# Three woven columns in an eight-batch Mamba, attention, GLA and MoE kernel: the front of batch t+2 issued during batch t's cycle

## The reference, cut to what matters

```
x = x + mamba(layernorm(x))         # the "scan part"
x = x + ffn(layernorm(x))           # attention, which only modulates a gated MLP
x = x + gla(layernorm(x))           # chunked gated linear attention, 8 chunks of 64
x = x + moe(layernorm(x))           # 32 experts, top 4

mamba: hidden, gate = split(x @ in_proj_w)         # 512 + 512 channels
       u = silu(conv4(hidden) + b)                 # causal, along the tokens
       dt, B, C = rms(split(u @ x_proj_w))         # 128, 16, 16
       dt = softplus(dt @ dt_proj_w + dt_proj_b)
       s_t = exp(dt_t * A) * s_{t-1} + dt_t * u_t * B_t      # 512 channels x 16 states
       y_t = sum over states of s_t * C_t
       out = ((y + u * D) * silu(gate)) @ out_proj_w
```

## Time and profile before

| | us |
|---|---|
| median of 3 runs | 3019.35 |
| lowest, highest | 3016.56, 3025.76 |
| span of the profiled execution | 2958.7 |
| PE busy in it | 2351.0 (79%) |
| DVE busy | 2163.5 (73%) |
| ACT busy | 1383.5 (47%) |
| POOL busy | 575.3 (19%) |

### The profile page before, as it was taken

The page is one execution under the profiler, slowest core; times in us unless marked ns, Lnnn a source line. Parts: engine busy times, 40 slices in busy tenths (PEclk is TensorE's granted clock), DMA queues, the critical chain, the costliest instruction groups (busy, mean ns, idle before and its releaser), DMA issues. The chain is left out here.

```text
span 2958.7 us, 36517 instructions
## 1 busy us (share of the span) xinstructions
PE 2351.0 (79%) x12305; PEld 1420.5 (48%) x12305; DVE 2163.5 (73%) x3017; ACT 1383.5 (47%) x2217; POOL 575.3 (19%) x569
## 2 busy tenths in 40 slices
PE   4448896889778977887788869787879688988991
PEld 2335354535453545444544545345535453556880
DVE  4993898489948894899669975998589852246666
ACT  5323654366535663566356634654465424143440
POOL 4000101120131013111311120212120230025661
PEclk8558897899889987998799979998999789988995
DMA  2320231023201321133113311231033182355757
GB/s 105 120 79 8 103 113 57 15 87 128 74 28 60 128 94 35 42 126 107 42 35 109 117 49 42 92 127 56 8 112 121 60 212 97 103 195 174 219 180 302
DMA packets 136229, 292.85 MB, mean 99 GB/s; under 512 B 14288, under 2 KB 79200, under 8 KB 135792
## 3 DMA queue, kind: packets, MB, share of 16 engines
q1 hardware_dynamic: 122224, 251.96, 26.2%
q0 software_dynamic: 13824, 38.55, 3.6%
HBM read 220.91 MB, written 69.54 MB: 98 GB/s over the span
## 5 line engine op out<-in xcount | busy, mean ns | idle before, releaser
L1367 DVE TENSOR_TENSOR_SCAN scan<-scan 128x1024 f32<-128x1024 f32 x256 | 585.9, 2289 | 34.4 <-ACT scan L1097 26.4
L2047 PE MATMUL bank<-ident,scan 128*128 128x128 f32 x2048 | 325.3, 315 | 168.9 <-DVE scan L1376 158.1
L1097 ACT ACTIVATE scan<-scan 128x511 f32<-128x511 f32 x512 | 337.2, 713 | 164.2 <-DVE scan L1367 163.5
L2047 PEld LDWEIGHTS bank<-ident,scan 128*128 128x128 f32 x2048 | 271.6, 162 | 260.1 <-DVE scan L1376 158.4
L1399 DVE TENSOR_TENSOR scan<-scan 128x1024 f32<-128x1024 f32 x256 | 310.5, 1213 | 29.5 <-PE bank L2047 28.5
L1376 DVE TENSOR_TENSOR scan<-scan 128x1024 f32<-128x1024 f32 x256 | 312.0, 1219 | 7.8 <-DVE rest L1579 7.5
L1936 PE MATMUL bank<-hT,wslot 128*128 128x512 f32 x512 | 246.9, 607 | 0.0
L1541 DVE TENSOR_REDUCE rest<-bank 128x2 f32<-128x1024 f32 (+3 forms) x176 | 196.5, 1126 | 66.5 <-PE bank L2118 63.5
L819 POOL DMA_INDIRECT rows_dram<-stage,slot_at x128 | 164.9, 1288 | 370.4 <-DVE scan L1367 313.1
L1144 ACT ACTIVATE rest<-bank 128x2048 f32<-128x2048 f32 (+3 forms) x128 | 158.2, 1236 | 146.7 <-PE bank L2138 146.6
L1936 PE MATMUL bank<-xT,scan 128*128 128x512 f32 (+1 forms) x352 | 185.0, 672 | 7.4 <-ACT xT L983 4.8
(11 more groups left out here) (341 smaller groups left out, 4231.2 us busy)
## 6 DMA issues: line engine op xcount, KB each, us to landing
scan<-bc_dram SPq DMA_DIRECT2D x256, 512.0 KB, 3.8
wslot<-wt SPq DMA_DIRECT2D x64, 384.0 KB, 3.5
rows_dram<-pad SPq DMA_DIRECT2D x32, 670.0 KB
scan<-y_dram SPq DMA_DIRECT2D x32, 512.0 KB, 10.1
rest<-rows_dram SPq DMA_DIRECT2D x108, 134.0 KB, 2.5
scan<-rows_dram SPq DMA_DIRECT2D x52, 134.0 KB, 2.7
scan<-wt SPq DMA_DIRECT2D x4, 1536.0 KB, 13.6
xa<-x SPq DMA_DIRECT2D x8, 512.0 KB, 3.8
```

The lines of the kernel that those rows point to most:

```text
L1097: i = a.activation(decay[:, unit % 2, n, 1:], dt[:, c, 1:], ACT.Exp, scale=a_neg[:, c, 2 * pair + n:2 * pair + n + 1])
L1367: d.tensor_tensor_scan(flat, decay[:, unit % 2].rearrange("p n t -> p (n t)"), flat, 0.0, ALU.mult, ALU.add).then_inc(decay_used.sem, 1)
L2047: m = t_.matmul(A.bank(("yT", c))[:, t * P:(t + 1) * P], drive[:, unit % NDRIVE, n, t * P:(t + 1) * P], ident[:, :], is_transpose=True, st ...
```

## The change

- The work is split into three columns per engine: U, the units of the scan; R, the rest part; X, the side: the out product of t (`out_part`), tiles 2 and 3 of the softplus and the gate products of t+1 (`gate_part`), the routing of t-1 (`late_alone`) and the front of t+2 (`front_part`: from the load of x to tiles 0 and 1 of dt). A single string of runs for each engine, `ORDER`, names the column and the number of steps, over all turns.
- The front no longer needs the drive buffers. Its tiles lie in `wslot` (`x_f`, `ssm`, softplus), so its load of x waits for the last down product of the MLP that used the slots (`down_done`), and the weights of the next MLP wait for the routing that uses them too. x is loaded a second time into `xa` as residual, 512 KB more for each batch.
- The convolution reads `hid` from PSUM, so its copy to SBUF and the memset go; DVE waits for ACT's first tap instead. `u` of tiles 2 and 3 is double-buffered; y goes into `sgate`; `bc_dram` is doubled.
- PSUM: front, gate, out and routing have rings of their own (F, G, O, K), all in banks 6 and 7 and handed from one to the next; A keeps the transposed y alone.
- The step counts of the U column on DVE are 102 for a turn, of the R column 122.

The core of the diff:

```diff
 def scan_jobs():
-    jobs = [("mT", c, "act") for c in range(NF)] + [("rt", 0, "dve")]
-    ...
-    jobs += [("out", i, "dve") for i in range(2)]
+    jobs = []
+    for c in range(0, NCT, 2): ... yT, y
+def front_jobs(): T, hid, ssm, dtT, bcT, dtp 0 and 1
+def gate_jobs(): dtp 2 and 3, gate
+        x_f = slots[:, 0:NT * HID].rearrange("p (t d) -> p t d", t=NT)
+        K = Ring(sem, "routing_bank", D, late_jobs())
+        F = Ring(sem, "front_bank", D, front_jobs())
+        G = Ring(sem, "gate_bank", D, gate_jobs())
+        O = Ring(sem, "out_bank", D, [(("out", i), "dve", 1) for i in range(2)])
 # SP
+            def front_in(turn):
+                yield
+                if turn >= 2:
+                    sp.wait_ge(down_done.sem, down_done.at(turn - 2, NFT))
+                ...
+                sp.dma_start(x_f, x[turn:turn + 1]...).then_inc(x_in.sem, 16)
 # DVE, convolution
-                        s = sv.step(d.scalar_tensor_tensor(dt[:, c], hid[:, c, k:k + SEQ], conv_w..., dt[:, c], ALU.mult, ALU.add)...)
+                    dve.wait_ge(fa.sem, fa.named(turn, f"tap{c}"))
+                    tile, b = u_of(turn, c), F.bank(("hid", c))
+                        i = d.scalar_tensor_tensor(tile[:, back:], b[:, 0:SEQ - back], conv_w..., tile[:, back:], ALU.mult, ALU.add)
 # DVE, columns
-            weave(rest_part(0), scan_part(1, None), ORDER["DVE"])
-            for turn in range(1, BATCH - 1):
-                weave(rest_part(turn), scan_part(turn + 1, turn - 1), ORDER["DVE"])
+            def side():
+                for turn in range(-1, BATCH):
+                    yield from out_part(turn) if turn >= 0 else idle(IDLE["DVE"]["O"])
+                    if turn < BATCH - 1:
+                        yield from late_alone(turn - 1, turn - 1, K) if turn >= 1 else idle(IDLE["DVE"]["L"])
+                        yield from front_part(turn + 2) if turn + 2 < BATCH else idle(IDLE["DVE"]["F"])
+                ...
+            weave(columns, ORDER["DVE"])
 # DVE, one cycle of the new string (t = 1 to 5 have the same)
+        "R19 X1 R4 X2 R4 X2 R10 X1 R6 X1 R9 X3 U1 X1 R1 X2 R1 U12 R2 U4 R1 X1 U4 R2 U12 X5 R4 X1 "
+        "R4 U1 R4 U1 R4 U1 R4 U1 R4 U1 R4 U1 R4 U1 R4 U1 R4 U1 R4 U1 R1 U1 R5 U51 R4 U4 R3 U1 R3 U1 R3 U1 "
```

More of the change, by code:

```diff
@@ L148, in unit_of, with weave, idle @@
     return u // 2, u % (2 * NPAIR) // 2, tile
[L151 to L158, removed]
-            pass
+def weave(columns, order):
+    for run in order.split():
+        for _ in range(int(run[1:])):
+            next(columns[run[0]], None)
+    for column in columns.values():
+        for _ in column:
+            pass
+def idle(steps):
+    for _ in range(steps):
+        yield
 RESIDENT = [
@@ L259, in before, with room, given_back @@
         return found
-    def room(self, turn, key):
+    def room(self, turn, key, handed=False):
         return [(self.freed[e].sem, self.freed[e].at(turn, self.count[i] + ago * self.freed[e].per))
-                for e, (ago, i) in self.before(key).items()]
+                for e, (ago, i) in self.before(key).items() if not (handed and ago)]
+    def given_back(self, turn, key):
+        return self.freed_sem(key), self.freed_at(turn, key)
 def rest_jobs():
@@ L850, in rest_part @@
+                    s = gp.step(g.tensor_tensor(dtu[:, c], sp_log(c), dtu[:, c], ALU.add).then_inc(gp.sem, 1))
+                    pool.wait_ge(gp.sem, gp.at(turn, s))
+                    marked(f"dt{c}", gp.step(g.tensor_tensor(dt[:, c], dt[:, c], dtu[:, c], ALU.add).then_inc(gp.sem, 1)))
             def rest_part(turn):
@@ new lines, in front_part @@
+                marked("ssm_sq", s)
+                if turn == 0:
+                    weights_made()
+                yield
+                if turn:
+                    act.wait_ge(gp.sem, gp.named(turn - 1, f"dt{NCT - 1}"))
+                empty(F, turn, ("dtT", 0), dtnT)
+                yield
+                empty(F, turn, ("bcT", 0), bcT, src=lambda b: b[0:2 * NSTATE, :])
+                for c in range(2):
+                    yield
+                    softplus(F, fa, turn, c)
+                yield
@@ L1077, in scan_part, with units @@
-                if late is not None:
-                    act.wait_ge(lv.sem, lv.named(late, "routed"))
+                    if turn and c == 0:
+                        act.wait_ge(O.ready.sem, O.filled_at(turn - 1, ("out", 1)))
+                    empty(G, turn, ("gate", c), sgate[:, c], ACT.Silu)
+            def units(turn):
                 for unit in range(NU):
@@ L1356, in scan_part, with units @@
+            def units(turn):
                 yield
+                uv.n = 0
                 drive_unit(turn, 0)
@@ L2094, in rest_part @@
                 yield
-                yield from token_product(B, turn, "v", xT, wv, HID, NF)
+                yield from token_product(B, turn, "v", [xT[:, c] for c in range(NF)], wv, HID, NF)
                 yield
@@ L2144, in rest_part @@
                             yield
+                            if w == 0:
+                                lent_to = [K.given_back(turn - 1, (n, 0)) for n in ("rt", "rank")] if 1 <= turn < BATCH - 1 else \
+                                    [G.given_back(1, ("gate", c)) for c in range(2, NCT)] if turn == 0 else \
+                                    [O.given_back(turn, ("out", 1))]
+                                handed(*lent_to)
                             pe.wait_ge(d_free.sem, d_free.at(turn, max(0, i - 1)))
@@ L2230, in rest_part @@
                 pe.wait_ge(B.freed_sem(("goT", 1)), B.freed_at(turn, ("goT", 1)))
-                yield from token_product(B, turn, "gout", goT, g_o, HID, NF)
+                yield from token_product(B, turn, "gout", [goT[:, c] for c in range(NF)], g_o, HID, NF)
                 yield
```

708 lines of the change are left out of this document (384 added, 324 removed), and 70 rows, old and new, of tables (LAST, ORDER).

## The result

The changed kernel takes 3295.05 us (median of four runs, 3288.88 to 3299.61) against 3022.56 for the kernel before in the same session: ratio 1.0894, 95% interval 1.087 to 1.0918, that is 272.5 us slower. In a later session it took 3258.22 against 2969.98, ratio 1.0973 (1.0952 to 1.0995).

A forecast was written before the change was run, and what follows sets the result against it. No engine was full over the whole (PE 79%, DVE 73%), so stages decide; a cycle of 202 + 148 = 350 us against 307.2 and the ends add 290 to 3019.35, forecast 3308 us, 8-in-10 range 3165 to 3395.

The forecast's parts named there:

- It doesn't do what it says: Order of cycles 1 to 5: the front stands beside the scan of t+1 in cycle 0 alone.
- A: Cycle from scan 0 to scan 31, units beside attention and routing: 202 us (190 to 208).
- the row maxima: 22 DVE row maxima in the stretch from scan 0 to scan 31: 24.6 us in all.
- The contention: POOL making dt 2 and 3 beside the first units slows DVE: 2 to 6 us, 5 taken.
- The table loads' 5 us: ACT's seven table loads ahead of decays that DVE waits for: 0 to 9 us, 5 taken.
- B: Cycle from gmod to the next scan 0, MLP plus GLA with the front, no units: 148 us (132 to 157).
- the rival with dearer handovers: Lower granted clock and all table loads reaching DVE: a cycle of 368 us, whole 3420; chance 0.12.
- tight nesting: Front and GLA fit into each other's waits, no stalls beside attention: cycle 321 to 335 us, whole 3150; chance 0.20.
- The removed copy and PSUM taps: Front's convolution: copy removed, three taps reading PSUM, costed at nothing, between -3 and +3 us in a cycle.
- The 60.7 around the span: Time outside the profiled span, 60.7 us, added to a span of 3249 to give 3309.
- the experts' stretch changed by more than 15 us: Sign named as showing the forecast wrong, on the experts' stretch.
- The other side: Front fills the hole at the cycle's head, units still cover MLP and GLA: cycle 280, whole 2830 us; chance 0.04.

The follow-up runs named there:

- interleaved kernel: Changed kernel with only the ORDER strings edited, units dealt out over the cycles, its own order from the last rest part on: 2946.27 us, ratio 0.9925; repeated 2946.08, 0.9922.
- eight units in the MLP: Changed kernel with units 24 to 31 of t+1 issued among the eight MLP tiles of t in cycles 1 to 5: 3230.64 us, ratio 1.0886.
- The kernel before in its second profile: Kernel before, unchanged, run and profiled once more in a later session: 3044.09 us with a span of 3042.3.

## Why the prediction was right, and where its terms were off

**The mechanism** held at each mark. Scan 0 of U1 came at 246.9 (245), cycle 0 took 342.0 (339), the following ones 347.5 (350), the last rest part began at 2669.5 (2676). The interleaved runs show that the written order is the cause, by taking it away. That it is the missing units beside the MLP and GLA alone they don't show: the interleaved kernel has only some nine of 32 units there and won all of the loss back, while eight units in the MLP won 7 us. "It doesn't do what it says", which I made the forecast itself, is what happened: the front of t+2 runs beside GLA, where no scan stands.

**A** was 211 where I had 202. The step that failed is the row maxima, taken at their busy 24.6 us alone. The rows that gave the busy time also give the idle time ahead of them, 5.2 + 1.6 + 0.4 waiting for PE; in A it is 9.9, in other cycles of the changed kernel 7.1 and 9.2. With the 2.1 of L1622 this is more than the whole miss. The contention was mis-sized a little: some 6.3 us (two units of about 7.6 against 4.45) for the 5. The wait for the logits was 2.2 (2). The table loads' 5 us were not there: no decay is among DVE's waits in A. DVE's work without the contention is 194.09 - 6.3 = 187.8 against my 190 and 186.

**B** was 137 where I had 148, and both parts were under. The MLP took 54.6, less than the 57.5 I took for its lower end: PE had 160 matmuls in it, 53.48 us, against 181 and 226 in the two stretches that I bounded it with the earlier trace rows. I had used turns in which other columns' products stood in the MLP, and the new order has hardly any there. GLA with the front took 82.5 against 89: the front's taps fill the waits of GLA (six of them, 4.55 us, stand between `kd` and the states), better than the two thirds of separate work that I charged. So A came out at the value of the rival with dearer handovers (210) and B inside that of tight nesting (132 to 141); the sum was near the forecast because they cancel, and that is luck. That the total was within 0.4% isn't a proof of its terms. Of the signs named, the cycle (345 to 355) and the full PE in the MLP came; DVE's share in the MLP was 18.8% for 20% to 25%, and GLA with the front 82.5 us for 85 to 95.

**The removed copy and PSUM taps**, costed at nothing between -3 and +3, have no price of their own in any run; the interleaved kernel has them and a cycle 2 to 4 us under that of before, so they can't cost much.

**The tables.** Two rows of ACT in GLA, a table load and what follows it:

```profile
1568.70 1.28 ACT L1343 ACT_TABLE_LOAD   x1
1569.99 0.63 ACT L1343 ACTIVATE rest<-rest 128x512 f32<-128x512 f32 x1
```

0.01 us lies between them, and the ACTIVATE ahead of the load ended 0.02 before it. The Trainium skill, "ScalarE: Activation LUTs", section "What ACT_TABLE_LOAD costs", would have some 1380 ns of drain at such a switch; the trace of after disagrees with it as that of before did.

**The sum.** "The 60.7 around the span" was wrong: 1.8 us lie around it (3293.45 against 3291.7). It did no harm, since from the median directly the sum was the same. The loss by medians is 272.5 in the first session and 288.2 in the last; I had 290. By the marks it is 274 to 288. And "the experts' stretch changed by more than 15 us" was a bad sign to name: it changed by 45 in the first profiles, and by 75 between two runs of the same kernel.

**The other side** (2830, units covering MLP and GLA as now) can come true in part, by another order: the interleaved kernel gains 25 us (2971.41 against 2946.27) in place of 189. It has fewer units there than the kernel before, some nine against 23 (11 in the MLP, 12 in GLA), and its cycle stops at 304, not 280. DVE has 243 us of work in it and PE 257, and each still waits for the other, as in the 26.7 us above; why 280 isn't reached was not tried.

## What to carry to other kernels

Before judging a reordering, list for each engine where its largest block of work stands after it and which engine is full there; with a block of 143 us of DVE beside attention alone a cycle took 44 us more than with the same columns in an interleaved order. Moving a part of the block into the hole isn't enough: eight units gave 7 us. Take a group's idle time into the sum together with its busy time when both stand in the same row. And compare kernels by marks at the start of stages, with the kernel before run again beside them: the last stretch of this one varies by 75 us without any change to it. The Trainium skill, "Perfetto Trace Analysis", section "Optimization Strategy", says that interleaving regimes with different busiest engines may help; the runs agree, with 348.2 against 304.0 us for a cycle.

## What was not expected of the hardware

**POOL beside DVE.** A scan of two SBUF operands takes 3.35 to 3.37 us in place of 2.29 and a product 2.22 in place of 1.20 while POOL's elementwise steps run: about 1.05 us more for each of the two lengths. The Trainium skill, "SBUF — State Buffer", section "Who interferes with whom", says that a DVE instruction with two SBUF inputs contends with a GpSimd instruction that reads SBUF, and calls the shared port pair an exclusive lock. The trace agrees for DVE, by 3.2 us for a unit. Both engines' instructions overlap in the records, and each DVE instruction is longer by about a microsecond, less than POOL's 1.90 to 3.13; whether that microsecond is a blocked piece the records don't tell, and POOL's own spans are rough.

**The clock is lower where PE has gaps.** The same 1350 matmuls of a cycle are 254 us at a granted clock of 0.89 in the kernel before, 257 at 0.91 in the interleaved one and 279 at 0.84 in the changed one. In A of the changed kernel, where PE waits 33.7 us for DVE's products by C, the granted clock was 0.78; in the MLP, with PE at 53.48 of 54.60, it was 1.00. So the changed kernel's PE is busy 22 us longer than the interleaved one's with the same products. That the waits are what lowers the clock fits these rows, but no run changed the one without the other.

**The last stretch.** The kernel before in its second profile spends 367.9 us from 2674.4 on, where the first profile has 292.7 from 2666.0. DVE's waits in that stretch of the slower run, which has 22.3 us in which it waited for nothing that the profile shows, 15 times:

```profile
DVE rest L1852 <- ACT rest L1264: 59.7, 47, 9.1
DVE rest L1852 <- issue: 22.3, 15, 4.9
```

In the quicker one the wait for ACT was 60.9 us in 89 pieces of at most 2.2, and that line has no row of the second kind there. What holds the engines there, and why it depends on the session, stays open: it was not tried.
